# An attention and mixture-of-experts kernel: keys from one product per half, arranged by transfers, and small sums moved to GpSimd

## The reference, cut to what matters

```python
# x: [16, 256, 128], ctx: [16, 64, 128], mask: [16, 64]; all float32
def xattn(H, T, mask):                     # 16 heads of 8, Lq = 256, Lkv = 64
    q, k, v = heads(H @ Wq) * 8 ** -0.5, heads(T @ Wk), heads(T @ Wv)
    s = q @ k.T + (1 - mask) * finfo.min   # per head
    return merge(softmax(s) @ v) @ Wo

def moe(x):                                # 4096 tokens, E = 8, F = 512, top 2, capacity 640
    probs = softmax(x @ gate_w.T); p, idx = top_k(probs, 2); p /= p.sum()
    for k in range(2):
        pos = rank of the token among those that chose the same expert as their k-th
        valid = pos < 640                  # later ones are dropped
        out += valid * p[k] * (silu(d @ wi_gate.T) * (d @ wi_up.T)) @ wo.T   # of its expert
    return out

x = x + xattn(layernorm(x), ctx, mask)
x = x + moe(layernorm(x))
```

## Time and profile before

| | |
|---|---|
| median of three runs | 383.05 us |
| the profiled execution's own time | 382.68 us |
| its span, first to last instruction | 380.7 us |
| outside the span | 2.0 us |
| instructions | 9057 |
| PE, DVE, ACT, POOL busy in the span | 345.0, 254.6, 193.7, 229.1 us |
| mean granted TensorE clock | 0.977 |

### The profile page before, as it was taken

How to read it: one execution, slowest core, us unless ns; L and a number is a source line. 1 busy time by engine, 2 the same in 40 slices (tenths; PEclk the granted TensorE clock), 3 DMA queues, 4 the chain that set the end, 5 groups by cost and what they waited for, 6 DMA issues and landing times.

```text
span 380.7 us, 9057 instructions
## 1 busy us (share of the span) xinstructions
PE 345.0 (91%) x3017; PEld 302.5 (79%) x3017; DVE 254.6 (67%) x981; ACT 193.7 (51%) x443; POOL 229.1 (60%) x195
## 2 busy tenths in 40 slices
PE   5889879898999997399999999999999999999970
PEld 1566667677877864288999999999999999999970
DVE  4999999999999997524455565645546455465440
ACT  3577777787878875224333444444434343443320
POOL 6383636575666567740663775755748748378663
PEclk9999999999999999689999999999999999999996
DMA  5898402222323121124237345363463643734232
GB/s 180 245 339 272 140 9 56 77 50 68 84 63 108 46 71 58 58 72 114 22 29 177 28 80 126 36 161 42 39 167 34 130 71 34 176 28 37 25 32 21
DMA packets 41158, 34.33 MB, mean 90 GB/s; under 512 B 8336, under 2 KB 37520, under 8 KB 40976
## 3 DMA queue, kind: packets, MB, share of 16 engines
q1 hardware_dynamic: 26592, 23.67, 21.4%
q0 software_dynamic: 13568, 9.58, 18.4%
q10 hardware_dynamic: 960, 0.60, 0.5%
HBM read 21.12 MB, written 17.73 MB: 102 GB/s over the span
## 4 chain that ended last, share of the span: by engine, by line
PE 64%; DVE 20%; issue 4%; POOL 4%; DMA 3%; ACT 2%; SPq 1%; POOLq 1%; DVEq 0%; ACTq 0%
PE bank L915 18%; PE bank L672 10%; PE bank L674 9%; PE bank L673 9%; DVE mneg L1021 5%; PE bank L775 5%; POOL slots L437 3%; PE bank L743 3%; PE bank L766 2%; DVE xn L1002 2%; DVE stats L988 2%; PE bank L906 2%; DVE rall L1071 2%; DMA maskr<-in_mask 1%; POOL out L471 1%
## 5 line engine op out<-in xcount | busy, mean ns | idle before, releaser
L471 POOL DMA_INDIRECT out<-ys,idx x80 | 125.4, 1568 | 82.2 <-DVE ys L1301 29.6
L1328 DVE TENSOR_TENSOR h<-sg,bank 128x256 f32<-128x256 f32 x160 | 66.0, 418 | 86.5 <-ACT sg L657 79.3
L657 ACT ACTIVATE sg<-bank 128x256 f32<-128x256 f32 x160 | 61.6, 385 | 107.2 <-PE bank L674 106.4
L672 PE MATMUL bank<-ex_hi,w_hi 128*128 128x256 f32 x320 | 95.5, 298 | 1.0
L674 PE MATMUL bank<-ex_lo,w_hi 128*128 128x256 f32 x320 | 89.1, 278 | 0.0
L673 PE MATMUL bank<-ex_hi,w_lo 128*128 128x256 f32 x320 | 89.0, 278 | 0.0
L437 POOL DMA_INDIRECT slots<-rall,slot x64 | 62.9, 983 | 34.0 <-DVE slot L1177 20.6
L915 PE MATMUL bank<-w_raw,h 128*128 128x128 f32 x640 | 78.0, 275 | 0.8 <-DVE h L1328 0.8
L915 PEld LDWEIGHTS bank<-w_raw,h 128*128 128x128 f32 x640 | 74.9, 192 | 1.0 <-DVE h L1328 1.0
L672 PEld LDWEIGHTS bank<-ex_hi,w_hi 128*128 128x128 f32 x320 | 60.3, 188 | 4.3 <-issue 2.5
L673 PEld LDWEIGHTS bank<-ex_hi,w_lo 128*128 128x128 f32 x320 | 60.4, 189 | 0.0
(11 more groups left out here) (122 smaller groups left out, 535.9 us busy)
## 6 DMA issues: line engine op xcount, KB each, us to landing
slots<-in_empty SPq DMA_DIRECT2D x8, 660.0 KB, 11.0
xl<-slots SPq DMA_DIRECT2D x7, 660.0 KB, 7.1
w_raw<-in_wgu SPq DMA_DIRECT2D x8, 512.0 KB, 3.8
w_raw<-in_wdn SPq DMA_DIRECT2D x8, 256.0 KB, 4.3
out<-X SPq DMA_DIRECT2D x16, 128.0 KB, 1.9
X<-in_x SPq DMA_DIRECT2D x3, 512.0 KB, 5.3
out<-ys,idx POOLq DMA_INDIRECT x80, 3.3
slots<-rall,slot POOLq DMA_INDIRECT x64
```

The source lines that it names most:

```text
L471: nc.gpsimd.indirect_dma_start(out=out[:, :], out_offset=bass.IndirectOffsetOnAxis(ap=IDX[v][:, j:j + 1], axis=0), in_=YS[c][:, t, :], in_ ...
L657: nc.scalar.activation(SG[m % 2][:], GATE_PS[m % 2][:, 0:2 * P], ACT.Silu).then_inc(sg_ready, 1)
L672: nc.tensor.matmul(ps, hi, m_hi, start=True, stop=False)
L1328: nc.vector.tensor_tensor(H[n % 2][:, f, :], SG[m % 2][:], UP_PS[m % 2][:, 0:2 * P], ALU.mult).then_inc(h_ready, 1)
```

## The change

Five things are changed.

1. **One product per half.** The key weights come once, 128 columns, ordered so that column 4c + g is channel c of group g. `project_keys(half)` is one `product3` with 128 rows; `keys_hi` and `keys_lo` run once for each half and write to CTXM and CTX_LO, the context tiles of that half, which nothing reads any more. Half 0 belongs to the start, half 1 to step 1. The mask and split of the second half of the context (`mask_context(1)`, `context_lo(1)`) move from the start into step 0.
2. **Copies by transfers.** Partition 4c + g has to go to row c of group g, three times. SP does it: six transfers for blocks 0 to 5 into a smaller KC (`arrange_keys`), ahead of the loads of X, and 12 transfers of 32 partitions by 10 blocks by 64 for blocks 6 to 15 into a new tile KL, plus four for its mask row, behind the experts' weights and ahead of `place_keys(3)`, which waits for all 16. Two of the four mask-row transfers of KC are issued by ScalarE.
3. **Variance constants.** The two adds of the constant move from VectorE to GpSimd, each right ahead of the power that reads it.
4. **Counts.** `added` is gone; `seen(m)` is two adds on GpSimd, behind the first send of step m + 3 and ahead of the other sends.
5. **The end.** In the last expert's last chunk, `down` stands behind piece 0 and `weigh` behind piece 1.

The diff, cut to its core (the removed `variance2` and `added`, and the lines of `moments` that went with VE, are not repeated):

```diff
-        K_PS = [MX[0], MX[1], DEN_PS, M1, M1, M1, M1, M1]
+        K_PS = M1
...
-            for g in range(GROUPS):
-                sp.dma_start(KC[ONE_ROW:ONE_ROW + 1, :, g, :], EXT[:]).then_inc(ext_in, 16)
+            for g in range(2):
+                sp.dma_start(KC[ONE_ROW:ONE_ROW + 1, g, :, :], EXT[0:KBUF, :]).then_inc(ext_in, 16)
+            def arrange_keys(piece):
+                b0, b1 = ((0, 2), (2, KBUF))[piece]
+                sp.wait_ge(k_used, 1)
+                for part in range(3):
+                    keys = CTXM[:, b0:b1, :] if part < 2 else CTX_LO[:, b0 * LK:b1 * LK].bitcast(F32)
+                    sp.dma_start(KC[32 * part:32 * part + 32, :, b0:b1, :], keys).then_inc(kc_in[piece], 16)
+            arrange_keys(0)
+            arrange_keys(1)
...
-            sp.wait_ge(k_used, 8)
-            sp.wait_ge(ext_in, 64)
+            sp.wait_ge(k_used, 2)
+            for part in range(3):
+                for g in range(GROUPS):
+                    keys = CTXM[g:P:GROUPS, KBUF:, :] if part < 2 else CTX_LO[g:P:GROUPS, KBUF * LK:].bitcast(F32)
+                    sp.dma_start(KL[32 * part:32 * part + 32, :, g, :], keys).then_inc(kl_in, 16)
+            for g in range(GROUPS):
+                sp.dma_start(KL[ONE_ROW:ONE_ROW + 1, :, g, :], EXT[KBUF:, :]).then_inc(kl_in, 16)
+            sp.wait_ge(kl_in, 16 * 16)
...
             def inverse_deviation2(i):
                 u = i % 2
+                pool.wait_ge(ln2_step, 2 * i + 2)
+                nc.gpsimd.tensor_scalar(VE2[u][:], MV2[u][:, :, 1], EPS, None, ALU.add).then_inc(ve2_ready, 1)
                 pool.wait_ge(ve2_ready, i + 1)
...
-            pool.wait_ge(k_used, 4)
+            pool.wait_ge(kc_in[0], 48)
...
+            def seen(m):
+                pool.wait_ge(rk_full, m + 1)
+                wait(pool, seen_ready, m)
+                oh = OH[m % 2][:].rearrange("p t k e -> p t (k e)")
+                nc.gpsimd.tensor_tensor(SEEN[:], SEEN[:], oh[:, 0], ALU.add).then_inc(count_step, 1)
+                pool.wait_ge(count_step, m + 1)
+                nc.gpsimd.tensor_tensor(SEEN[:], SEEN[:], oh[:, 1], ALU.add).then_inc(seen_ready, 1)
...
-            def keys_lo(n):
-                half, g = n // 4, n % 4
-                dve.wait_ge(k_hi, n + 1)
-                lo = KC[64:96, 8 * half:8 * half + 8, g, :]
-                nc.vector.tensor_tensor(lo.bitcast(F32R), K_PS[n][64:96, :].rearrange("p (b k) -> p b k", k=LK), lo, ALU.subtract).then_inc(k_used, 1)
+            def keys_lo(half):
+                dve.wait_ge(k_hi, half + 1)
+                nc.vector.tensor_tensor(CTX_LO[:, 512 * half:512 * half + 512], K_PS[:],
+                                        CTXM[:, 8 * half:8 * half + 8, :].rearrange("p b k -> p (b k)"), ALU.subtract).then_inc(k_used, 1)
...
-                            if f == 1 and c > 0:
+                            if f == (0 if last and v == 1 and c == NC - 1 else 1) and c > 0:
                                 down(it, n - 1, v)
```

134 lines of the change are left out of this document (57 added, 77 removed).

## The result

The changed kernel takes 388.43 us (median of three runs, 387.13 to 389.08) where the kernel before takes 383.05: 1.0142 times as long, with an interval of 1.0115 to 1.0168. The forecast was 380.7, with a range of 378.6 to 385.2. It was wrong in sign. Medians are of all runs of a kernel; ratios, with a 95% interval, leave single slow runs out.

The account below looks back on a forecast made before the run. TensorE was taken as the bound, with VectorE's removed work paying only where VectorE is late. Terms -2.0 - 0.3 - 1.2 + 0.5 + 1.3 - 0.5 = -2.2 us on 382.68 gave 380.5, forecast as 380.7, range 378.6 to 385.2.

Parts of the forecast that it names:

- The start: Up to step 2: less VectorE work brings step 3's row maximum 2.4 us sooner, less 0.4 in step 2: -2.0 us.
- The late keys: Blocks 6 and 7: keys placed from KL come at 66.9 us, just behind their need; charged +0.5 us.
- The tail: GpSimd's last sends of part 1, from 152 us: counts and constants among them and later powers cost +1.3 us.
- The end: Last expert's last chunk: the fourth output product starts 0.47 us sooner, and GpSimd's transfers with it; -0.5 us.
- The mask product in step 0: VectorE's second mask product, moved into step 0 behind a key spread: 0.69 to 2.21 us, 1.5 taken.
- the second norm in step 2: VectorE's norm behind GpSimd's spread of block 5's keys, with GpSimd taking the port again: +0.4 us, from 0 to 1.
- Steps 3 to 7: VectorE loses constant and counts: -0.3 us in step 3, -1.2 from shorter waits at the moments of steps 5 and 7.
- the wait for the row maximum: Fourth row scores of steps 5 and 7: waits of 1.05 us shrink by 0.6 each, to about 0.5.
- rival A: Late keys decide: block 6's keys come at 72 to 77 us, total 386 to 390, mild case 384; chance 0.20.
- a pair of counts: Two count adds on GpSimd among the tail's sends: 0.35 us taken for a pair.
- Rival B: GpSimd's small work takes all the gain: pairs 1.0 us, constants 0.6 each; total 383.6, at half 382.2; chance 0.18.
- the empty queue: SP's transfer queue, full with fills and experts' weights, is empty at about 46.3 us; KL's transfers move behind it.

Follow-up runs that it names:

- c1: The changed kernel with five more TensorE products, read by nobody, in its idle gap of the start; 401.29 us beside 409.23 for the kernel before, ratio 0.983.
- g2: The changed kernel with counts and constants on VectorE and ScalarE's two mask-row issues behind its first copies; 383.33 us, ratio 1.0005 to the kernel before.
- d1: The kernel before with only the counts and variance constants moved to GpSimd, keys and end untouched; 387.20 us, ratio 1.0115.
- e4: The changed kernel with counts and constants back on VectorE, leaving the keys' change and the end; 384.45 us, ratio 1.005 to the kernel before.

## Why the prediction was wrong, step by step

The forecast was 2.2 us down and the span went 5.9 up. Of the 8.1 between them 3.8 are the start, 2.5 the eleven steps behind it with the late keys, 1.5 the tail, and 0.3 the end.

**The start, -2.4 and +0.4 in the forecast, +1.78 at the first rank.** The step that failed is a term put at nothing without a word: the clock was taken as full. The change takes TensorE's work of the keys out of the very place where it covered the wait for the norm (before, six products lie between 11.0 and 12.6 us, and TensorE waits 0.32; now it waits 2.68), and nothing in the forecast asked what an emptier TensorE does to the clock. It was at half for 13.7 us. Where it stayed full (c1) the row maximum came at 36.02 and the first rank 2.2 us sooner than before, and the forecast had 36 and 2.0: the count of work was right, though such close agreement is partly luck, since two profiles of the kernel before differ by 0.64 us here.

The gap was there to be read. ScalarE's two issues were in the text (they set the transfers to 12.0 us, and they came at 12.10), but I took "the first queries run through TensorE and ScalarE, neither of which is shortened on that way" as the end of it and didn't follow what else stood behind the issues: keys' copy, low part, norm, turn. The first turn did not come later by it (12.73, before 12.91), but it could have come at 10.43 (g2), and TensorE had nothing else to do. The mask product in step 0 took 1.79 us at 24.07, under GpSimd's spread of 23.41 to 25.31, as forecast (0.69 to 2.21, 1.5 taken); the second norm in step 2 took 2.18 for its pair against 1.91, +0.27 (forecast +0.4).

**Steps 3 to 7, -0.3 and -1.2; measured +0.6.** Between the first and the second rank the step went from 8.61 to 8.30, the forecast 0.3. The steps with moments went from 8.59 and 8.57 to 9.02 each, and the wait for the row maximum, forecast to shrink to 0.5, is still there:

```profile
74.90 0.50 PE L774 MATMUL bank<-ks,qs 97*128 97x256 f32 x2 [1.05 <-DVE mneg L1046]
```

"In these steps GpSimd's own add comes ahead of its power, and the result is needed about 0.3 us after it is there now; at 0.2 us for the add nothing is late" failed. I had asked when the power's result is needed, not what loop the power stands in. VectorE's lead of 0.26 us a step could not grow, because its second norm waits for GpSimd (0.25 to 0.69 us in four of the steps from 88 us on). With both back on VectorE the steps are 8.57 and 8.70.

**Beyond step 7, not in the forecast: +0.9.** I gave the steady steps no cost, because TensorE had 7.26 us and GpSimd 64% of its time in work. A loop over two engines has no share of busy time; it needs its own sum. Before, it was 3.5 for the three sends, 0.05, 0.72 for the power and 2.7 from there to the next slots, 7.0 us: 0.3 under TensorE's 7.26, and a constant takes 0.45. Of the 0.9 us, 0.60 is one step, the one behind the last moments (7.84 for 7.24; d1 has the same 7.84). There the chain is GpSimd's alone from 94.08 to 98.58 us: both constants, both powers, the late send and the pair of counts, all ahead of the three sends. This is where counts on top of constants cost something.

**The late keys, +0.5; measured 0.** SyncE began to place keys at 56.13 us, where the forecast had KL there at 53.0. Its issues for KL began at 38.00 and not at 33.6, when the late start had brought the low part of the second keys; and of the eight issues of high parts three took 1.50, 3.10 and 2.59 us, the others 0.62 to 0.87, so that the last of the sixteen ended at 55.06. The keys of block 6 came about 2 us later than the forecast's 66.9, but so did their need, so that they came with room to spare. In g2, where the start is sooner, they came at about 67.0 and cost 2.13 us of wait; rival A had them at 72 to 77. SyncE's issues in the changed kernel:

```profile
38.00 11.19 SPq L359 DMA_DIRECT2D kl<-ctxm  x8
49.23 2.60 SPq L359 DMA_DIRECT2D kl<-ctx_lo  x4
51.87 3.19 SPq L361 DMA_DIRECT2D kl<-ext  x4
56.13 23.71 SPq L342 DMA_DIRECT2D ks<-kl  x32
```

**The tail, +1.3; measured +1.30 in the last four steps and +1.52 behind them.** The mechanism was right and the terms too small: a pair of counts is 0.42 and 0.53 us (0.35 forecast) and the constant 0.33 (0.2). From the send behind the last power to the last send it is 11.76 us, before 10.25 (156.55 to 166.80): two pairs make 1.0 of these 1.5 us, and the other 0.5 is one send of 1.47 us in place of 0.96, which the forecast did not have at all. It belongs to the small instructions on GpSimd: all 11 profiles with counts or constants there have one such send (1.47 to 1.90), the 9 without have none. Its cause was not tried. And each of the last four steps, not three, waits for the power.

**The end, -0.5; measured -0.4.** Right.

Rival B came nearest in its mechanism, since GpSimd's small work took it all and more; but I gave it a price per instruction, and not per turn of a loop. By the times, counts and constants are 3.9 us (d1), and the start and the keys 1.6 (e4) with the end's 0.4 taken off already; together 5.5 of the 5.4 measured.

Three small sums of the forecast do not come out, and nothing hangs on them: 15.8 us and 30 us of transfers give 45.8 for the empty queue, not 46.3; rival A's far end is 391, not 390; and the parts of the chances add up to 0.59 faster and 0.22 slower.

## What to carry to other kernels

Before a small instruction is moved to an idle engine, follow the loop in which its result stands (here slot, sends, power, norm, slot) and add up that loop; an engine busy for 64% of the time can be the bound. Where a change takes products out of TensorE's start, look at what covered each wait there, and allow for the clock: here 6.8 to 13.7 us at half cost 3 to 4 us. And when a queue's issues move to a compute engine, everything behind them on that engine moves too.
